# Joining the output weights in another order in a decoder layer's prologue, one core of a Trainium2 chip

## The chip, the cores and the metric

The kernel runs on one core of one Trainium2 chip. A core has TensorE (PE, matmul; its weight loads are listed apart as PEld), VectorE (DVE), ScalarE (ACT), GpSimd (POOL) and SyncE (SP), which here only issues DMAs. The metric is the device time of one execution in microseconds (us); less is better.

## What is computed

A decoder layer over 16 batches of 100 tokens of width 512, in float32: a sliding-window attention with a learned sink, a cross attention over a context, and a mixture of 32 experts (top 4) with a shared expert. The part that matters here is how the attention's output is projected, and what it normalises first:

```
h = layernorm(x)
q = h @ wq_comp @ wq_up                     # 16 heads of 128
k = rmsnorm(rope(h @ wk)) ; v = h @ wv
attn = softmax(mask(q k^T) with sink) @ v
x1 = einsum('btgi,gio->btgo', attn as 4 groups of 512, out_w1)   # 4 groups
x1 = x1.reshape(b, t, 2048) @ out_w2        # (2048, 512)
x  = x + x1
...
x = x + cross_attention(layernorm(x), ctx)
x = x + experts(layernorm(x))
```

## The kernel before

Since nothing stands between `out_w1` and `out_w2`, the kernel multiplies the two once, ahead of the batches. This is the prologue. For each of 16 heads n a "join" makes a 128 x 512 product of four matmuls of 512 columns in bank n % 4 of the PSUM tensor W; ScalarE copies it to `wch` (the high half, counted by the semaphore `high`), VectorE subtracts to get `wcl` (the low half, counted by `low`), and TensorE counts finished joins on `wc_ps`. Joins 4g to 4g+3 need weight group g (2 MB: `w1T[g]` and `out_w2`'s rows). Groups 0 and 2 are loaded into the tile `w_x`, groups 1 and 3 into the tile `work` (the list `half`, L228). Join n waits for `low` of n - 3, as its bank must be free.

`work` also holds the attention's working tiles: the transposed queries `T16`, the probabilities `Pm` and `PX`, the rotated queries `qr`, and the normalised rows `h1`, `h2`. `resid` holds x for all 16 batches.

After the prologue `pipeline` runs `step(b)` on every engine. Step b does stage A for batch b (attention scores, softmax, output projection), stage Q for batch b + 1 (layer norm 1, compressed queries, keys, values, rotation), stage X for batch b - 1 (cross attention) and stage C for batch b - 2 (router). Step 0 has A for batch 0 and Q for batch 1. Batch 0's own Q stage stands in the prologue: `ln1_columns(0)` (four transposes of h1 into PSUM), `compress(0)`, `queries(0)` on TensorE, with `rotate_keys`, `rotate`, `norms`, `scale_keys` on VectorE and `squares` on ScalarE.

Each engine takes its instructions in the written order and waits in place. So does SP: its DMAs are issued in the order of its program, and a wait ahead of one holds back all behind it. SP's order is: group 0, x of batch 0, 14 constants, group 1, three attention weights; wait for 4 joins; group 2, x of batches 1 to 15; wait for 8 joins; group 3; wait for 12 joins; the cross attention's weights and the router (semaphore `ld_wx`); then three fills of DRAM (`pad_st`): the table of expert lists (L293), and zeros behind the rows of `hx_rows` (L294) and `out_rows` (L295); then the context of each step.

Layer norm 1 of batch b + 1 goes over three engines in step b. VectorE makes mean and variance (`ln_stats`, L1003 to L1007), GpSimd raises to the power -1/2 (`ln1`, L1323), VectorE applies it (`ln1_apply`, L1012). GpSimd's program begins so:

```python
wait_alone(pool, s.wqk, 1)
ln1(0)
qk(0)
pool.wait_ge(s.pad_st, 48)
pipeline(pool, step)
```

The wait on `pad_st` stands ahead of step 0's `ln1(1)`, and is met when all three fills have landed.

Of the kernel before, what the change touches and what calls it, by code (L numbers as in the profile page):

```python
# [8 lines left out]
NH, D = 16, 128  # L9
# [8 lines left out]
QH = 4  # L18
# [73 lines left out]
def build(nc, a, out):  # L92

    with ExitStack() as ctx:
# [132 lines left out]

        half = [[w_x[:, 0:2048], w_x[:, 2048:4096]], [work[:, 0:2048], work[:, 2048:4096]]]  # L228
        block = ctx.enter_context(nc.Block())
# [32 lines left out]
        def _(sp):  # L262
# [5 lines left out]
            for g in range(G):  # L268

                if g >= 2:  # L270
                    sp.wait_ge(s.wc_ps, 4 * (g - 1))
                h, done = half[g % 2], (s.ld_half0, s.ld_half1)[g % 2]
                sp.dma_start(h[0].rearrange("p (k n) -> p k n", k=4),
                             a["w1T"][g].rearrange("(k p) n -> p k n", p=P)).then_inc(done, 16)
                sp.dma_start(h[1].rearrange("p (k n) -> p k n", k=4),
                             a["out_w2"][GI * g:GI * (g + 1), :].rearrange("(k p) n -> p k n", p=P)).then_inc(done, 16)
                if g == 0:
                    sp.dma_start(rv[:, 0:1, :], xv[:, 0:1, :]).then_inc(s.ld_x0, 16)
                    for t, n in consts:
                        sp.dma_start(t[:, :], a[n]).then_inc(s.ld_const, 16)  # L280
                if g == 1:
                    for t, n, k in ((w_comp, "wq_comp", KC), (w_up, "wq_up", 1), (w_kv, "wkv", KC)):
                        sp.dma_start(t[:, :].rearrange("p (k n) -> p k n", k=k),
                                     a[n].rearrange("(k p) n -> p k n", p=P)).then_inc(s.ld_w, 16)
                if g == 2:
                    sp.dma_start(rv[:, 1:NB, :], xv[:, 1:NB, :]).then_inc(s.ld_x, 16)
            sp.wait_ge(s.wc_ps, 4 * (G - 1))
            for t, n, k in ((w_q, "WqT", KC), (w_kx, "WkvT", 1), (w_out, "WoutT", KC), (w_r, "routerT", KC)):
                sp.dma_start(t.rearrange("p (k n) -> p k n", k=k) if n != "routerT" else
                             t[:, :].rearrange("p (k n) -> p k n", k=k),  # L290
                             a[n].rearrange("(k p) n -> p k n", p=P)).then_inc(s.ld_wx, 16)

            sp.dma_start(table, a["c_table"]).then_inc(s.pad_st, 16)  # L293
            sp.dma_start(hx[NTOK:ROWS, :], a["c_zero"]).then_inc(s.pad_st, 16)  # L294
# [76 lines left out]
        def _(pe):  # L371
# [7 lines left out]

            def join(g):  # L380
                pe.wait_ge((s.ld_half0, s.ld_half1)[g % 2], 32 * (g // 2 + 1))
                for i in range(4):
                    n = 4 * g + i
                    if n >= 4:
                        pe.wait_ge(s.low, n - 3)
                    if n == 14:
                        pe.wait_ge(s.kv, 1)
# [10 lines left out]

            def ln1_columns(c):

                pe.wait_ge(s.ln1_h, c + 1)
                to_columns(wb[0], h1).then_inc(s.h1T_ps, 1)

            def compress(c):

                pe.wait_ge(s.h1T, c + 1)
                for k in range(KC):
                    last = mm(wb[1][:, 0:T], w_comp[:, P * k:P * (k + 1)], h1T[:, T * k:T * (k + 1)],
                              start=k == 0, stop=k == KC - 1)
                last.then_inc(s.hq_ps, 1)  # L410
                for k in range(KC):
                    last = mm(wb[2][0:T, 0:2 * D], h1T[:, T * k:T * (k + 1)], w_kv[:, 256 * k:256 * (k + 1)],
                              start=k == 0, stop=k == KC - 1)
                last.then_inc(s.kv_ps, 1)
# [15 lines left out]
            def step(b):  # L430
# [50 lines left out]
                if do.Q:  # L481
                    ln1_columns(b + 1)
                if do.X:
# [15 lines left out]
                if do.Q:  # L499
                    compress(b + 1)  # L500
                    pe.wait_ge(s.s_scaled, 4 * b + 4)
# [81 lines left out]

            for g in range(G - 1):
                join(g)
            pe.wait_ge(s.ld_const, 16 * 14)
            pe.wait_ge(s.ld_w, 48)
            pe.wait_ge(s.low, 4 * (G - 1))
            ln1_columns(0)
            compress(0)  # L590
            queries(0)
            join(G - 1)
            pe.wait_ge(s.low, 4 * G)
            pe.wait_ge(s.ld_wx, 64)
            pe.wait_ge(s.h1T, 1)
            pipeline(pe, step)
# [133 lines left out]
        def _(act):  # L730
# [10 lines left out]

            def ln1_columns(c):
                act.wait_ge(s.h1T_ps, c + 1)
                act.wait_ge(s.kv_ps, c)
                copy(h1T[:, :], wb[0][:, 0:QW]).then_inc(s.h1T, 1)

            def compressed(c):
                act.wait_ge(s.hq_ps, c + 1)
                act.wait_ge(s.q_ps, 4 * c)
                copy(hqT[:, :], wb[1][:, 0:T]).then_inc(s.hqT, 1)  # L750
# [3 lines left out]
                copy(kvs[:, :], wb[2][0:T, 0:2 * D]).then_inc(s.kv, 1)  # L754

# [29 lines left out]
            def step(b):  # L785
# [13 lines left out]
                if do.X:  # L799
# [10 lines left out]
                    copy(qpT[:, :], wb[1][:, 0:QW]).then_inc(s.qp, 1)  # L810
                if do.Q:
                    ln1_columns(b + 1)
                if do.A:
# [3 lines left out]
                    act.wait_ge(s.p_den, 2 * b)  # L817
                    fn(esink[:, :], sdiff[:, :], ACT.Exp).then_inc(s.e_sink, 1)
                if do.X:
                    act.wait_ge(s.sx_ps, b)  # L820
# [4 lines left out]
                if do.Q:  # L825
                    compressed(b + 1)
                    key_square(b + 1)
# [36 lines left out]

            joined(range(0, 12))
            ln1_columns(0)
            compressed(0)
            key_square(0)
            squares_first(0)
            queries_out(0)  # L870
            squares(0)
            joined(range(12, 16))
            pipeline(act, step)
# [105 lines left out]
        def _(dve):  # L979
# [74 lines left out]
            def step(b):  # L1054
                do = stages(b)
                if do.Q:
                    if isinstance(b, int) and b == 0:
                        dve.wait_ge(s.ld_x, 16)
                    ln_stats(0, b + 1, s.ln1_stats, s.ln1_var)
# [17 lines left out]
                if do.A:  # L1077
                    dve.wait_ge(s.s_max, 2 * b + 2)
                    tt(P3, P3, per_head(mx[:, :], NH), ALU.subtract).then_inc(s.s_shift, 1)
                    tt(sdiff[:, :], sink[:, :], mx[:, :], ALU.subtract).then_inc(s.s_sink, 1)  # L1080
                if do.C:

# [119 lines left out]
            ln1_apply(0)  # L1202
            joined(range(0, 12))
            rotate_keys(0)
            rotate(0)
            norms(0)
            scale_keys(0)
            joined(range(12, 16))
            pipeline(dve, step)
# [271 lines left out]
```

## Time and profile before

| | us |
|---|---|
| median of 3 runs | 1243.26 (1242.33 to 1248.41) |
| the profiled execution's own time | 1251.86 |
| its span (first to last instruction) | 1250.0 |
| TensorE busy | 1156.1 (92% of the span) |
| VectorE busy | 812.8 (65%) |
| ScalarE busy | 593.8 (48%) |
| GpSimd busy | 370.6 (30%) |

Times in the rows are counted from the span's start. The profiled execution is 8.6 us longer than the median of the runs, so differences are worked out on the profile and laid on either time.

### The profile page before, as it was taken

Reading aid. Unit: us, or ns where it says so; the run is one execution under the profiler, and the core shown is the slowest. Engines: PE = TensorE matmul, PEld = TensorE weight load, DVE = VectorE, ACT = ScalarE, POOL = GpSimd, SP = SyncE. Lnnn points to the kernel's source line nnn. Section 1 sums busy time; section 2 is a strip of 40 time slices with the busy share of each in tenths; the row PEclk is TensorE's granted clock in tenths of the full one; section 3 lists DMA queues with packets and bytes.
Section 4 is the critical chain, followed back from the end, with each engine's and each line's share of the span. In section 5 each row is a group of like instructions: output and inputs, shape, how many; then the busy total and the mean of one; then the engine's idle time right before and its main releaser. Section 6 shows DMA issues by size and latency. Waiting matters only on the chain. (4 is left out here: it accounts for less than half of the span.)

```text
span 1250.0 us, 20961 instructions
## 1 busy us (share of the span) xinstructions
PE 1156.1 (92%) x7761; PEld 911.6 (73%) x7762; DVE 812.8 (65%) x1392; ACT 593.8 (48%) x1402; POOL 370.6 (30%) x279
## 2 busy tenths in 40 slices
PE   7989999999999999999999874899989999999992
PEld 3456677767776777677767653888779988889992
DVE  1155698789878988898889754532266666655660
ACT  1234554465445554555456422411156666656661
POOL 0011102212221222121212111401226566665662
PEclk9989999999999999999999895899989999989997
DMA  7910000000000000000000008202569999999964
GB/s 267 244 72 2 1 9 9 15 14 8 9 15 14 8 9 15 14 8 9 15 14 8 10 14 219 67 27 63 181 210 274 267 271 268 272 264 246 267 116 59
DMA packets 70459, 121.10 MB, mean 97 GB/s; under 512 B 18502, under 2 KB 22134, under 8 KB 70250
## 3 DMA queue, kind: packets, MB, share of 16 engines
q1 hardware_dynamic: 52682, 82.46, 20.4%
q0 software_dynamic: 17728, 37.97, 14.6%
q8 instruction: 33, 0.54, 0.2%
q14 instruction: 16, 0.13, 0.0%
HBM read 93.55 MB, written 28.13 MB: 97 GB/s over the span
## 5 line engine op out<-in xcount | busy, mean ns | idle before, releaser
L1323 POOL TENSOR_TENSOR rall<-qkv_var,phalf 100x17 f32<-100x17 f32 x16 | 49.2, 3074 | 415.4 <-DVE qkv_var L1046 415.4
L1389 POOL DMA_INDIRECT out_rows<-work,idx x64 | 127.9, 1998 | 113.4 <-issue 87.2
L375 PE MATMUL QS<-xh,wh 128*128 128x256 f32 x512 | 148.6, 290 | 0.0
L376 PE MATMUL QS<-xl,wh 128*128 128x256 f32 x512 | 146.0, 285 | 0.0
L377 PE MATMUL QS<-xh,wl 128*128 128x256 f32 x512 | 145.9, 285 | 0.0
L375 PE MATMUL W<-wch,oth 128*100 128x512 f32 x256 | 104.9, 410 | 0.0
L376 PE MATMUL W<-wcl,oth 128*100 128x512 f32 x256 | 100.7, 393 | 0.0
L377 PE MATMUL W<-wch,otl 128*100 128x512 f32 x256 | 100.4, 392 | 0.0
L376 PEld LDWEIGHTS QS<-xl,wh 128*128 128x128 f32 x512 | 99.4, 194 | 1.2
L375 PEld LDWEIGHTS QS<-xh,wh 128*128 128x128 f32 x512 | 99.4, 194 | 1.2
L377 PEld LDWEIGHTS QS<-xh,wl 128*128 128x128 f32 x512 | 99.2, 194 | 0.0
L1271 DVE TENSOR_TENSOR wl<-raw,wh 128x2048 fp32r<-128x2048 f32 (+1 forms) x48 | 84.5, 1760 | 12.6 <-ACT wh L734 12.2
L1323 POOL TENSOR_TENSOR rstd<-var,phalf 100x1 f32<-100x1 f32 (+1 forms) x48 | 30.4, 632 | 201.9 <-DVE var L1007 127.1
L1353 POOL DMA_INDIRECT expert_lists<-tok,slot x64 | 74.3, 1161 | 24.2 <-issue 18.4
L1292 DVE TENSOR_TENSOR work<-work,QS 128x256 f32<-128x256 f32 x64 | 26.8, 418 | 76.2 <-ACT work L946 74.2
L734 ACT ACTIVATE wh<-raw 128x2048 fp32r<-128x2048 f32 (+1 forms) x48 | 70.8, 1475 | 0.0
L734 ACT ACTIVATE work<-W 128x400 f32<-128x400 f32 (+1 forms) x128 | 54.2, 509 | 31.7 <-PE W L515 31.6
L478 PEld LDWEIGHTS W<-h2T,w_x 128*128 128x128 f32 x512 | 59.7, 192 | 8.0 <-issue 7.5
L926 ACT ACTIVATE work<-W,wcol 128x512 f32<-128x512 f32 x64 | 40.6, 686 | 46.7 <-PE W L377 43.0
L580 PE MATMUL W<-w_x,oxT 128*100 128x512 f32 x128 | 60.8, 619 | 0.0
L734 ACT ACTIVATE work<-QS 100x400 f32<-100x400 f32 (+1 forms) x80 | 43.8, 611 | 34.1 <-DVE work L1038 23.3
L478 PE MATMUL W<-h2T,w_x 128*128 128x100 f32 x512 | 59.4, 274 | 0.0
(206 smaller groups left out, 2874.8 us busy)
## 6 DMA issues: line engine op xcount, KB each, us to landing
raw<-in_w SPq DMA_DIRECT2D x24, 1024.0 KB
raw<-in_w SPq DMA_DIRECT2D x24, 512.0 KB
work<-in_w SPq DMA_DIRECT2D x8, 1024.0 KB
work<-in_w SPq DMA_DIRECT2D x8, 512.0 KB
hx_rows<-h3x SPq DMA_DIRECT2D x16, 212.5 KB
h_columns<-h3s SPq DMA_DIRECT2D x16, 200.0 KB, 1.9
h3T<-h_columns SPq DMA_DIRECT2D x16, 200.0 KB, 4.7
out_rows<-ytiles POOLq DMA_DIRECT2D x16, 200.0 KB, 2.5
```

What stands on the lines that cost most here:

```text
L375: mm(dst, ah, bh, start=start, stop=False)
L376: mm(dst, ah, bl, start=False, stop=False)
L377: return mm(dst, al, bh, start=False, stop=stop)
L478: last = mm(wb[1][:, T * i:T * (i + 1)], w_q[:, 512 * k + P * i:512 * k + P * (i + 1)], h2T[:, T * k:T * (k + 1)], start=k == 0, stop=k == ...
L580: last = mm(wb[3][0:T, :], oxT[:, T * k:T * (k + 1)], w_out[:, 512 * k:512 * (k + 1)], start=k == 0, stop=k == KC - 1)
L734: return fn(dst, src, ACT.Copy)
L926: last = fn(Y[e % 2][:, 512 * j:512 * (j + 1)], wb[j][:, :], ACT.Copy, scale=wcol[e % RING][:, j:j + 1])
L1271: tt(wl[e % 2][:, c], slots_w[e % RING][:, c], wh[e % 2][:, c].bitcast(fp32), ALU.subtract).then_inc(m.wl, 1)
L1292: tt(ea[:, 256 * v:256 * (v + 1)], et[:, 256 * v:256 * (v + 1)], QS[:, 1280 + 512 * v:1536 + 512 * v], ALU.mult).then_inc(m.act, 1)
L1323: return nc.gpsimd.tensor_tensor(out=dst, in0=src, in1=phalf[:, 0:src.shape[1]], op=ALU.pow)
L1353: nc.gpsimd.indirect_dma_start(table, on_rows(slot[:, k:k + 1]), tok[:, :], None)\
L1389: nc.gpsimd.indirect_dma_start(out, on_rows(idx[:, NE * j + e:NE * j + e + 1]), Y[e % 2][:, 512 * j:512 * (j + 1)], None, compute_op=ALU.a ...
```

## The change

Four things are done together.

1. Weight groups 1 and 3 no longer land in `work`, but in the places of x's rows 8 to 15 in `resid` (columns 4096 to 8191). So `work` is free for batch 0 while joins run.
2. x is loaded in two parts. Batches 1 to 7 are issued right after group 1 and the attention weights, with no wait. Batches 8 to 15 are issued when all 16 joins are done (`wc_ps` at NH = 16, since the last group lies in their place), after the cross attention's weights.
3. Batch 0's Q stage goes among the joins, in the banks of QS in place of W: its transposes after join 7, `compress(0)` after join 8, `queries(0)` after join 9. VectorE's and ScalarE's parts are put between their halves of the joins.
4. Joins 14 and 15 go from the prologue into step 0, after its scores on TensorE. Their evictions stand on ScalarE on both sides of the softmax's exponentials, and on VectorE behind the softmax's subtraction.

The diff, without the passing of banks as arguments:

```diff
-        half = [[w_x[:, 0:2048], w_x[:, 2048:4096]], [work[:, 0:2048], work[:, 2048:4096]]]
+        half = [[t[:, 0:2048], t[:, 2048:4096]] for t in (w_x, resid[:, HID * NB // 2:HID * NB])]
@@ SP
-                if g == 2:
-                    sp.dma_start(rv[:, 1:NB, :], xv[:, 1:NB, :]).then_inc(s.ld_x, 16)
+                if g == 1:
+                    sp.dma_start(rv[:, 1:NB // 2, :], xv[:, 1:NB // 2, :]).then_inc(s.ld_x, 16)
             sp.wait_ge(s.wc_ps, 4 * (G - 1))
...
+            sp.wait_ge(s.ld_x, 16)
+            sp.wait_ge(s.wc_ps, NH)
+            sp.dma_start(rv[:, NB // 2:NB, :], xv[:, NB // 2:NB, :]).then_inc(s.ld_x, 16)
             sp.dma_start(table, a["c_table"]).then_inc(s.pad_st, 16)
             sp.dma_start(hx[NTOK:ROWS, :], a["c_zero"]).then_inc(s.pad_st, 16)
             sp.dma_start(out[NTOK:ROWS, :], a["c_zero"][:, 0:HID]).then_inc(s.pad_st, 16)
@@ PE, step
                 if do.Q:
-                    ln1_columns(b + 1)
+                    if isinstance(b, int) and b == 0:
+                        pe.wait_ge(s.qT, QH)
+                        join(range(14, 16))
+                    ln1_columns(b + 1, wb[0])
...
                 if do.Q:
-                    compress(b + 1)
+                    if isinstance(b, int) and b == 0:
+                        pe.wait_ge(s.low, NH)
+                    compress(b + 1, wb)
@@ PE, prologue
-            for g in range(G - 1):
-                join(g)
+            join(range(0, 8))
             pe.wait_ge(s.ld_const, 16 * 14)
+            ln1_columns(0, qb[0])
+            join(range(8, 9))
             pe.wait_ge(s.ld_w, 48)
-            pe.wait_ge(s.low, 4 * (G - 1))
-            ln1_columns(0)
-            compress(0)
+            compress(0, qb)
+            join(range(9, 10))
+            pe.wait_ge(s.kv, 1)
             queries(0)
-            join(G - 1)
-            pe.wait_ge(s.low, 4 * G)
+            join(range(10, 14))
+            pe.wait_ge(s.low, 14)
             pe.wait_ge(s.ld_wx, 64)
-            pe.wait_ge(s.h1T, 1)
             pipeline(pe, step)
@@ ACT, step
-                if do.Q:
-                    ln1_columns(b + 1)
+                first = isinstance(b, int) and b == 0
+                if first:
+                    joined(range(14, 15))
+                if do.Q and not first:
+                    ln1_columns(b + 1, wb[0])
                 if do.A:
                     act.wait_ge(s.s_shift, b + 1)
                     fn(Pm[0:T, :], Pm[0:T, :], ACT.Exp).then_inc(s.p_exp, 1)
                     act.wait_ge(s.s_sink, b + 1)
                     act.wait_ge(s.p_den, 2 * b)
                     fn(esink[:, :], sdiff[:, :], ACT.Exp).then_inc(s.e_sink, 1)
+                if first:
+                    joined(range(15, 16))
+                    ln1_columns(b + 1, wb[0])
@@ DVE, step
-                    if isinstance(b, int) and b == 0:
-                        dve.wait_ge(s.ld_x, 16)
+                    if isinstance(b, int) and b < 2:
+                        dve.wait_ge(s.ld_x, 16 * (b + 1))
...
                     tt(sdiff[:, :], sink[:, :], mx[:, :], ALU.subtract).then_inc(s.s_sink, 1)
+                    if isinstance(b, int) and b == 0:
+                        joined(range(14, 16))
```

What SP issues from group 2 on, before the change (the brackets are the semaphores that a row waits for):

```order
L273 DMA w_x<-in_w1T 128x4x512 [waits wc_ps]
L275 DMA w_x<-in_out_w 128x4x512
L286 DMA resid<-in_x 100x15x512
L273 DMA work<-in_w1T 128x4x512 [waits wc_ps]
L275 DMA work<-in_out_w 128x4x512
L289 DMA w_x<-in_WqT 128x4x512 [waits wc_ps]
L289 DMA w_x<-in_WkvT 128x1024
L289 DMA w_x<-in_WoutT 128x4x512
L289 DMA w_r<-in_routerT 128x4x32
L293 DMA expert_lists<-in_c_table 16x3328
L294 DMA hx_rows<-in_c_zero 16x8704
L295 DMA out_rows<-in_c_zero 256x512
```

And after it, from the same place:

```order
L286 DMA resid<-in_x 100x7x512
L273 DMA w_x<-in_w1T 128x4x512 [waits wc_ps]
L275 DMA w_x<-in_out_w 128x4x512
L273 DMA resid<-in_w1T 128x4x512 [waits wc_ps]
L275 DMA resid<-in_out_w 128x4x512
L289 DMA w_x<-in_WqT 128x4x512 [waits wc_ps]
L289 DMA w_x<-in_WkvT 128x1024
L289 DMA w_x<-in_WoutT 128x4x512
L289 DMA w_r<-in_routerT 128x4x32
L295 DMA resid<-in_x 100x8x512 [waits wc_ps,ld_x]
L296 DMA expert_lists<-in_c_table 16x3328
L297 DMA hx_rows<-in_c_zero 16x8704
```

The zeros of `out_rows` come next (L298). The three fills now stand behind x of batches 8 to 15 and its wait for the sixteenth join.

TensorE from the end of the prologue, through the scores of step 0, before the change:

```order
L390 MATMUL W<-work 128x512 [waits low]
L390 MATMUL W<-work 128x512 x3
L438 MATMUL QS<-ident,kr 128x100 [waits k_scaled,h1T,q_rot,ld_wx,low]
L449 MATMUL W<-ident,work 128x100 x16
L455 MATMUL QS<-mask_115,identb 100x400 [waits qT,kT]
```

Behind those scores, before the change:

```order
L458 MATMUL QS<-kT,work 100x100 x4
L396 MATMUL W<-ident,work 128x100 [waits ln1_h]
L396 MATMUL W<-ident,work 128x100 x3
L408 MATMUL W<-h1T,w_comp 128x100 [waits h1T]
L408 MATMUL W<-h1T,w_comp 128x100 x3
L412 MATMUL W<-w_kv,h1T 100x256 x4
```

And after the change, in the same place:

```order
L460 MATMUL QS<-kT,work 100x100 x4
L392 MATMUL W<-resid 128x512 [waits low,ld_half1,qT]
L392 MATMUL W<-resid 128x512 x3
L392 MATMUL W<-resid 128x512 [waits low,ld_half1]
L392 MATMUL W<-resid 128x512 x3
L398 MATMUL W<-ident,work 128x100 [waits ln1_h]
L398 MATMUL W<-ident,work 128x100 x3
L410 MATMUL W<-h1T,w_comp 128x100 [waits h1T,low]
L410 MATMUL W<-h1T,w_comp 128x100 x3
L414 MATMUL W<-w_kv,h1T 100x256 x4
```

The two last joins now stand between batch 0's scores and batch 1's transposes, and the compression waits for `low` too.

GpSimd's first rows after the change, which are those of before with other line numbers:

```order
L1344 TENSOR_TENSOR rstd_88<-var_85,phalf 100x1 [waits ln1_var]
L1344 TENSOR_TENSOR rall<-qkv_var,phalf 100x17 [waits s_scaled,qk_var]
L1344 TENSOR_TENSOR rstd_88<-var_85,phalf 100x1 [waits ln1_var,pad_st]
L1344 TENSOR_TENSOR rall<-qkv_var,phalf 100x17 [waits s_scaled,qk_var]
L1344 TENSOR_TENSOR rstd_89<-var_86,phalf 100x1 [waits ln2_var]
```

The third row is batch 1's layer norm. Nothing moved here; its wait for the fills is unchanged.

## Rows read from the trace of the kernel before

**Rows 1.** Busy time by stretch: start:end, length, engines (instructions), PE clock, DMA share, GB/s.

```profile
140.00:600.00 460.00, 458.30 (x3369) 336.57 (x3369) 385.06 (x715) 246.02 (x771) 94.79 (x84) 1.00 0.04 11
```

**Rows 2.** Timeline of TensorE: start, length, line, tiles, records [idle before <-releaser].

```profile
39.28 13.90 PE L390 MATMUL W<-w_x 128*128 128x512 f32 x32
...
54.79 0.53 PE L396 MATMUL W<-ident,work 100*128 100x100 f32 x4 [1.62 <-DVE wcl L997]
...
63.59 13.90 PE L390 MATMUL W<-work 128*128 128x512 f32 x32
78.90 0.30 PE L438 MATMUL QS<-ident,kr 100*128 100x100 f32 x1 [1.41 <-DVE wcl L997]
...
83.21 0.87 PE L458 MATMUL QS<-kT,work 128*100 128x100 f32 x8
87.27 0.93 PE L396 MATMUL W<-ident,work 100*128 100x100 f32 x4 [3.19 <-DVE work L1012]
88.80 2.03 PE L408 MATMUL W<-h1T,w_comp 128*128 128x100 f32 x8 [0.59 <-ACT h1T L734]
...
93.65 3.60 PE L419 MATMUL QS<-w_up,hqT 128*100 128x512 f32 x8
97.08 1.54 PE L515 MATMUL W<-ident,work 100*100 100x100 f32 x16
...
127.52 1.14 PE L408 MATMUL W<-h1T,w_comp 128*128 128x100 f32 x8
...
130.22 3.60 PE L419 MATMUL QS<-w_up,hqT 128*100 128x512 f32 x8
```

**Rows 3.** Timeline of SP: start and length of the issue of a DMA.

```profile
39.47 0.37 SPq L273 DMA_DIRECT2D work<-in_w1T  x1
...
53.20 0.37 SPq L289 DMA_DIRECT2D w_x<-in_WqT  x1
...
63.02 0.59 SPq L295 DMA_DIRECT2D out_rows<-in_c_zero  x1
```

**Rows 4.** DMA issues, 0 to 90 us: count, KB each, median us to landing.

```profile
resid<-in_x SPq DMA_DIRECT2D x1, 3000.0 KB
...
w_x<-in_out_w SPq DMA_DIRECT2D x2, 1024.0 KB, 7.6
...
hx_rows<-in_c_zero SPq DMA_DIRECT2D x1, 544.0 KB, 5.6
...
out_rows<-in_c_zero SPq DMA_DIRECT2D x1, 512.0 KB, 8.6
```

**Rows 5.** Busy time by stretch in the prologue and step 0, columns as in the first group.

```profile
23.00:24.00 1.00, 1.00 (x4) 0.52 (x3) 0.64 (x1) 0.00 (x0) 0.00 (x0) 1.00 0.00 0
34.00:41.00 7.00, 7.00 (x18) 3.04 (x17) 1.38 (x2) 1.20 (x2) 0.00 (x0) 1.00 0.66 136
51.00:54.00 3.00, 2.17 (x6) 0.63 (x4) 0.26 (x2) 0.60 (x1) 0.00 (x0) 1.00 0.67 214
56.00:62.00 6.00, 6.00 (x21) 4.30 (x22) 0.69 (x5) 1.83 (x11) 0.00 (x0) 0.74 1.04 392
88.00:93.00 5.00, 4.41 (x16) 3.52 (x15) 3.38 (x6) 2.40 (x4) 0.00 (x0) 0.50 0.02 5
```

**Rows 6.** Timeline of GpSimd around batch 1's layer norm.

```profile
80.10 0.56 POOL L1323 TENSOR_TENSOR rstd<-var,phalf 100x1 f32<-100x1 f32 x1 [5.97 <-DVE var L1007]
```

**Rows 7.** Timeline of VectorE there.

```profile
86.67 0.54 DVE L1012 TENSOR_SCALAR work<-resid,mv,rstd 100x512 f32<-100x512 f32 x1
```

**Rows 8.** Timeline of ScalarE there.

```profile
77.52 0.60 ACT L734 ACTIVATE wch<-W 128x512 fp32r<-128x512 f32 x1 [2.83 <-PE W L390]
...
88.24 0.50 ACT L734 ACTIVATE h1T<-W 128x400 f32<-128x400 f32 x1 [6.97 <-PE W L396]
88.98 1.54 ACT L815 ACTIVATE work<-work 100x1600 f32<-100x1600 f32 x1 [0.24 <-DVE work L1079]
90.42 0.20 ACT L818 ACTIVATE esink<-sdiff 100x16 f32<-100x16 f32 x1
```

More of the change, by code:

```diff
@@ L377, in split_product, with join @@
                 return mm(dst, al, bh, start=False, stop=stop)
[L380 to L383, printed above, removed]
+            def join(heads):
+                for n in heads:
+                    g, i = n // 4, n % 4
+                    pe.wait_ge((s.ld_half0, s.ld_half1)[g % 2], 32 * (g // 2 + 1))
                     if n >= 4:
                         pe.wait_ge(s.low, n - 3)
-                    if n == 14:
-                        pe.wait_ge(s.kv, 1)
                     for k in range(4):
@@ L397, in to_columns, with ln1_columns, compress @@
                 return last
-            def ln1_columns(c):
+            def ln1_columns(c, bank):
                 pe.wait_ge(s.ln1_h, c + 1)
-                to_columns(wb[0], h1).then_inc(s.h1T_ps, 1)
-            def compress(c):
+                to_columns(bank, h1).then_inc(s.h1T_ps, 1)
+            def compress(c, banks):
                 pe.wait_ge(s.h1T, c + 1)
                 for k in range(KC):
-                    last = mm(wb[1][:, 0:T], w_comp[:, P * k:P * (k + 1)], h1T[:, T * k:T * (k + 1)],
+                    last = mm(banks[1][:, 0:T], w_comp[:, P * k:P * (k + 1)], h1T[:, T * k:T * (k + 1)],
                               start=k == 0, stop=k == KC - 1)
@@ L411, in compress @@
                 for k in range(KC):
-                    last = mm(wb[2][0:T, 0:2 * D], h1T[:, T * k:T * (k + 1)], w_kv[:, 256 * k:256 * (k + 1)],
+                    last = mm(banks[2][0:T, 0:2 * D], h1T[:, T * k:T * (k + 1)], w_kv[:, 256 * k:256 * (k + 1)],
                               start=k == 0, stop=k == KC - 1)
@@ L740, in joined, with ln1_columns, compressed @@
                     copy(wch[:, 512 * n:512 * (n + 1)], wb[n % 4]).then_inc(s.high, 1)
-            def ln1_columns(c):
+            def ln1_columns(c, bank):
                 act.wait_ge(s.h1T_ps, c + 1)
                 act.wait_ge(s.kv_ps, c)
-                copy(h1T[:, :], wb[0][:, 0:QW]).then_inc(s.h1T, 1)
-            def compressed(c):
+                copy(h1T[:, :], bank[:, 0:QW]).then_inc(s.h1T, 1)
+            def compressed(c, banks):
                 act.wait_ge(s.hq_ps, c + 1)
                 act.wait_ge(s.q_ps, 4 * c)
-                copy(hqT[:, :], wb[1][:, 0:T]).then_inc(s.hqT, 1)
+                copy(hqT[:, :], banks[1][:, 0:T]).then_inc(s.hqT, 1)
                 act.wait_ge(s.kv_ps, c + 1)
@@ L753, in compressed @@
                 act.wait_ge(s.k_rot, c)
[L754 removed]
+                copy(kvs[:, :], banks[2][0:T, 0:2 * D]).then_inc(s.kv, 1)
             def queries_out(c):
@@ L825, in step @@
                 if do.Q:
-                    compressed(b + 1)
+                    compressed(b + 1, wb)
                     key_square(b + 1)
@@ L863, in step @@
                     copy(oxT[:, :], wb[1][:, 0:QW]).then_inc(s.oxT, 1)
-            joined(range(0, 12))
-            ln1_columns(0)
-            compressed(0)
+            joined(range(0, 8))
+            ln1_columns(0, qb[0])
+            joined(range(8, 9))
+            compressed(0, qb)
             key_square(0)
+            joined(range(9, 10))
             squares_first(0)
             queries_out(0)
+            joined(range(10, 11))
             squares(0)
-            joined(range(12, 16))
+            joined(range(11, 14))
             pipeline(act, step)
@@ L1202, in _ @@
             ln1_apply(0)
-            joined(range(0, 12))
+            joined(range(0, 9))
             rotate_keys(0)
+            joined(range(9, 10))
             rotate(0)
+            joined(range(10, 12))
             norms(0)
+            joined(range(12, 13))
             scale_keys(0)
-            joined(range(12, 16))
+            joined(range(13, 14))
             pipeline(dve, step)
```

## The prediction

> **What bounds the kernel now.** I read the busy time by stretch first, then TensorE's timeline over the prologue and step 0, then what SP issues and when it lands, and last the three engines that make batch 1's layer norm. In the loop over the batches TensorE is busy 458.3 of 460 us [rows 1]: each step is paced by TensorE, the steps follow each other without slack, and so what moves the start of the steady run moves the end by as much. The change touches only what lies ahead of it. Nothing behind step 1 is altered, so I follow one milestone: the start of step 0's probability transposes, 97.08 us before [rows 2]. From there on the work is the same.
>
> How that milestone comes about now: joins 8 to 11 run back to back from 39.28, 3.43 us each (each group of four is 13.90 long with its tail, and starts of one kind repeat that spacing) [rows 2]. Then batch 0's Q stage stands alone, with joins held back until 63.59, so it costs about 10.4 us of TensorE's time; joins 12 to 15 follow, and step 0 starts at 78.90. Its scores end at 84.08. TensorE then idles until VectorE has applied batch 1's layer norm (86.67) and starts its transposes at 87.27, compression at 88.80, queries at 93.65 [rows 2, 7]. In 88 to 93 us it had the clock at 0.50, the 1.2 GHz level [rows 5].
>
> **What the change takes away.** With Q among the joins no join waits for it. TensorE's work up to the end of join 11 is then 39.28 + four joins (13.73) + columns (0.5) + compression at the full clock (127.52 to 130.22: 2.70) + queries (93.65 to 97.08: 3.43) = 59.6 us [rows 2]. Joins 12 and 13 take it to 66.5. Step 0 started 1.4 us behind its last join before [rows 2], which gives 67.9. VectorE and ScalarE keep up: a join's eviction is 0.60 us [rows 8] against 3.43 of a join, and what they do for Q takes about as long as before and lies under three to four joins.
>
> Step 0 also waits for the cross attention's weights. They were issued at 53.20, behind the twelfth join [rows 3], and will be at 59.6. A pair of 1 MB loads with nothing in front needs 8.0 us from the first issue (0.4 to the second, 7.6 to landing) [rows 4]; the four loads hold 0.6 MB more, 1.5 us at 392 GB/s [rows 5]. They land at about 69.1, so step 0 starts at 69.2, 9.7 us earlier than now. TensorE has idled 2.7 us by then, near the 3.19 us behind which the half clock stood before [rows 2, 5]; I take it that the clock falls and costs 2 us over the next four (at either level known: 0 or 2). Scores end at 69.2 + 5.2 + 2 = 76.4, joins 14 and 15 at 83.3.
>
> The early load of x and the new places of groups 1 and 3 I cost at nothing. x of batches 1 to 7 (7/15 of 3000 KB, 1.43 MB [rows 4]) is now in front of group 2, and even at 136 GB/s [rows 5] takes 10.5 us. The loads up to the attention weights are through before 23 us, where the DMA share is 0.00 [rows 5]; x starts there, group 2 gets the engines that x uses at 33 and needs 5.4 us at 392 GB/s more: about 38.5, and join 8 wants it at 39.8. If this cover of 1.3 us is missing, the excess is paid once. Group 3 no longer stands behind x and has 12 us to spare.
>
> **What the change adds.** The step that I follow closely is SP's. The three fills were issued just behind the cross weights, the last at 63.02, landed 8.6 us later at 71.6 [rows 3, 4], and GpSimd, which waits for them ahead of batch 1's power, ran it at 80.10 as soon as VectorE's variance was there [rows 6]: the wait cost nothing. Now the fills stand behind x of batches 8 to 15, and that waits for the sixteenth join, which is inside step 0. So at 83.3 us SP issues x, then the fills. From issue to full landing there are: 2.7 us of start and completion (the pair above, 8.0 us less 2.1 MB at 392 GB/s); x, 1.64 MB; the fills, 544 and 512 KB and a table of 16 x 3328 words, 1.29 MB, 3.3 us at 392 GB/s [rows 4, 5]. x loads go slower than others: alone from 34 to 41 us the core moved 136 GB/s with a DMA share of 0.66, that is 10.6 of 16 engines, and 214 with 0.67 from 51 to 54 [rows 5]. I weigh the two by their length, 159 GB/s, so x takes 10.3 us (7.7 to 12.0). The fills must be whole on all engines, those that x holds too. They have landed at 83.3 + 2.7 + 10.3 + 3.3 = 99.6.
>
> The Trainium skill (DMA: Bandwidth & Descriptors, Specifications) gives about 27 GiB/s for one DMA engine. Ten engines would carry x at some 290 GB/s, an estimate from that page, and x would take 5.7 us in place of 10.3; the sum below would be 12.2 in place of 16.8. The rows of x, 13.6 to 21.4 GB/s on an engine, do not reach that.
>
> Queued behind it: GpSimd cannot make batch 1's power (0.56 us), VectorE waits in place for it with the softmax's subtraction of batch 0 behind, ScalarE with the exponentials behind that, TensorE with the transposes. Batch 1's layer norm is applied at 99.6 + 0.56 + 0.15 = 100.3 in place of 86.67: +13.6 [rows 6, 7].
>
> From there the way is longer too. Before, compression began 2.1 us behind the layer norm (86.67 to 88.80) [rows 2, 7], with h1T copied ahead of the exponentials (88.24, then 88.98) [rows 8]. Now ScalarE copies h1T behind them: subtraction as before, so exponentials 2.3 us behind the layer norm, 1.64 us for both, join 15's eviction 0.60, h1T 0.50 [rows 8], 0.2 of handing over: 5.2 us. That adds 3.1. TensorE is cold, as before (0.50 from 88 to 93 [rows 5]), so compression and queries cost the same 8.3 us. Join 15's low half on VectorE ends just with h1T and delays nothing more; the softmax's last multiplication ends some 4 us ahead of the transposes.
>
> **The sum.** 13.6 + 3.1 = +16.7, with rounding +16.8: the milestone goes from 97.1 to 113.9. On the profiled execution, span 1250.0 and own time 1251.86, that is 1268.7; on the median, 1243.26, it is 1260.1. The 8.6 us between the two are the profiled execution's own and are not in my forecast, which is 1260 us.
>
> **Rivals.**
> *Faster, the reordering pays.* If GpSimd's wait did not come last, TensorE would go on at 83.3 with the transposes; join 15's eviction, h1T and its low half let the compression start at 84.6, warm, 2.70 and 3.43 later the milestone stands at 90.7: -6.4, 1236.9 us. What speaks for it is that TensorE's stand-alone Q stage does vanish. It needs the fills landed by about 82.8, where +0 lies at 83.5 for the layer norm's start plus 13.6; they are issued at 83.3 at the earliest. It decides only if the fills are not behind the join. The order rows say that they are. Within 0.5% needs the fills by 89.
> *x runs fast.* If the ten engines carry x at the rate of one in the full stream, 392/16 = 24.5 GB/s each [rows 5], x takes 6.7 us and the sum is 13.2, 1256.5. Of x's own rows none shows it. This is also where the page's figure would lead. If in addition the clock does not fall in front of step 0, it is 11.2, 1254.5.
> *The transfers collide.* If group 2 is late for join 8 by 2 us, and the fills need the 8.6 us of their landing before in place of 6.0, the sum is 16.8 + 2 + 2.6 = 21.4, 1264.7.
> *All near the best.* x and the fills at 392 GB/s with the clock kept: 7.5 + 2.7 us from 81.3, the sum is 8.7, 1252.0.
>
> **How the numbers follow.** Forecast 0.62; x fast 0.16; collision 0.11; all near the best 0.04; faster 0.03; less than 0.5% either way, by a landing that I cannot derive, 0.04. The range is 1252 to 1266: it takes in the bounds of x's rate, both levels of the clock and the collision. What a measurement can tell here is about 0.5%, 6.2 us, so faster 0.03, within it 0.04, slower 0.93.
>
> **What would show it.** In the changed kernel's profile: joins without a pause from 8.7 to about 66 us; step 0's first matmul near 69; x and the fills issued at about 83; GpSimd's second small power idle until about 100, with VectorE's layer norm right behind it; TensorE idle from 83 to 101 and cold after; the transposes near 114. I am wrong if that power runs before 90, or if the span behind it is longer or shorter than before.

## The result, and the profile after

The changed kernel is slower: 1264.46 us (median of 4 runs, 1261.77 to 1267.32) against 1242.8 us (4 runs, 1235.7 to 1248.41); the ratio is 1.0178, 95% interval 1.0119 to 1.0237. The ratios here and below leave out every execution more than 1.5% above the fastest of its kernel, so they need not be the quotient of the medians. By this ratio the change costs 22 us (15 to 29). Its profiled execution took 1266.37 us, with a span of 1264.5, 14.5 more than the profiled one of before. The forecast was 1260, in a range of 1252 to 1266.

First TensorE's timeline, the same stretch as [rows 2]:

```profile
38.72 0.51 PE L398 MATMUL QS<-ident,work 100*128 100x100 f32 x4
...
42.52 1.03 PE L410 MATMUL QS<-h1T,w_comp 128*128 128x100 f32 x8
...
48.55 3.60 PE L421 MATMUL QS<-w_up,hqT 128*100 128x512 f32 x8
...
58.85 7.03 PE L392 MATMUL W<-resid 128*128 128x512 f32 x16
68.76 0.40 PE L440 MATMUL QS<-ident,kr 100*128 100x100 f32 x1 [2.88 <-issue]
68.95 2.87 PE L451 MATMUL W<-ident,work 100*128 100x100 f32 x16
...
76.61 7.05 PE L392 MATMUL W<-resid 128*128 128x512 f32 x16
100.64 0.93 PE L398 MATMUL W<-ident,work 100*128 100x100 f32 x4 [16.98 <-DVE work L1028]
105.26 2.03 PE L410 MATMUL W<-h1T,w_comp 128*128 128x100 f32 x8 [3.69 <-DVE wcl L1013]
...
109.69 3.60 PE L421 MATMUL QS<-w_up,hqT 128*100 128x512 f32 x8
113.13 1.54 PE L522 MATMUL W<-ident,work 100*100 100x100 f32 x16
```

Read it in two halves. Up to 83.7 the change does what it says: batch 0's queries lie among the joins, no join waits, and step 0 starts at 68.76 where it started at 78.90 [rows 2]. Then TensorE stands still for 17 us, until VectorE has applied the layer norm. The milestone of the prediction, the start of step 0's probability transposes, is at 113.13 in place of 97.08.

Why VectorE is late stands one engine further, in the queues of SP and GpSimd and in VectorE's own timeline:

```profile
83.75 0.32 SPq L295 DMA_DIRECT2D resid<-in_x  x1
84.11 0.68 SPq L296 DMA_DIRECT2D expert_lists<-in_c_table  x1
84.83 0.57 SPq L297 DMA_DIRECT2D hx_rows<-in_c_zero  x1
85.45 0.59 SPq L298 DMA_DIRECT2D out_rows<-in_c_zero  x1
```

```profile
99.45 0.56 POOL L1344 TENSOR_TENSOR rstd<-var,phalf 100x1 f32<-100x1 f32 x1 [35.41 <-DMA out_rows<-in_c_zero]
```

```profile
68.20 0.15 DVE L1023 TENSOR_SCALAR var<-mv 100x1 f32<-100x1 f32 x1
...
100.04 0.55 DVE L1028 TENSOR_SCALAR work<-resid,mv,rstd 100x512 f32<-100x512 f32 x1 [20.60 <-POOL rstd L1344]
100.50 1.82 DVE L1095 TENSOR_TENSOR work<-work,mx 100x1600 f32<-100x1600 f32 x1
...
104.51 0.69 DVE L1013 TENSOR_TENSOR wcl<-W,wch 128x512 fp32r<-128x512 f32 x1 [1.51 <-ACT wch L741]
```

The variance was ready at 68.35. GpSimd's power of 0.56 us could have run then; it ran at 99.45, and its releaser is the last of the three fills, `out_rows<-in_c_zero`. In [rows 6] the same instruction was released by VectorE's variance at 80.10. From the issue of x at 83.75 to the power are 15.7 us. What the engines and the DMA did in them, and ScalarE behind them:

```profile
84.00:99.00 15.00, 0.00 (x0) 0.00 (x0) 0.00 (x0) 0.00 (x0) 0.00 (x0) 0.65 0.67 199
```

```profile
102.36 1.54 ACT L825 ACTIVATE work<-work 100x1600 f32<-100x1600 f32 x1 [21.49 <-DVE work L1095]
103.80 0.20 ACT L828 ACTIVATE esink<-sdiff 100x16 f32<-100x16 f32 x1
103.90 0.58 ACT L741 ACTIVATE wch<-W 128x512 fp32r<-128x512 f32 x1
104.38 0.50 ACT L741 ACTIVATE h1T<-W 128x400 f32<-128x400 f32 x1
```

No engine computes anything for 15 us while 3 MB are moved. Behind it ScalarE makes h1T only after the exponentials and join 15's eviction, and VectorE's half of join 15 stands behind that eviction too. Compression starts 5.2 us behind the layer norm (100.04 to 105.26), where it was 2.1. What ends its wait is join 15's low half (104.51 and 0.69 long, up to 105.20); h1T was ready 0.3 us earlier.

### The profile page after: what moved, and what is told of

It reads as the page before. It is cut to its first block and busy times, and to the rows that moved or that the text cites. A ratio compares the mean times of both kernels' runs of the same rounds, so it can differ in the third digit from the quotient of the medians.

```text
span 1264.5 us, 20973 instructions
## 1 busy us (share of the span) xinstructions
PE 1158.4 (92%) x7761; PEld 915.0 (72%) x7762; DVE 812.1 (64%) x1392; ACT 594.3 (47%) x1402; POOL 360.5 (29%) x279
## 3 DMA queue, kind: packets, MB, share of 16 engines
q1 hardware_dynamic: 52692, 82.46, 20.2%
## 5 line engine op out<-in xcount | busy, mean ns | idle before, releaser
L1410 POOL DMA_INDIRECT out_rows<-work,idx x64 | 121.8, 1904 | 123.4 <-issue 81.8
```

What stands on the lines that cost most here:

```text
L1410: nc.gpsimd.indirect_dma_start(out, on_rows(idx[:, NE * j + e:NE * j + e + 1]), Y[e % 2][:, 512 * j:512 * (j + 1)], None, compute_op=ALU.a ...
```

## The experiments

The theory (A): all of the loss comes from the fills' new place in SP's queue, behind the sixteenth join and x, since GpSimd waits for them ahead of batch 1's layer norm. Against it: the joins inside step 0 and their evictions are what costs (B); something behind the milestone costs too (C); the transfers disturb, not the wait (E). Three smaller questions go with them: do the fills delay the cross weights (D), do the fills alone take the time from issue to power (F), and does the milestone of before vary by chance (G).

The table has each kernel's milestone, the same instruction's start in the last full step (15), and the total. The profile of before had 97.08 and 710.32, that of the changed kernel 113.13 and 726.38. The kernels were timed in three groups, each beside the kernel before, and the ratio is to before in the same group. Before had a median of 1244.19 us (29 runs) in the first group (changed again, fills first, GpSimd waits later, before with the second half of x and the fills late), 1243.44 (29) in the second (before again, fills between, weights' wait later, joins in prologue) and 1247.64 (7) in the third (evictions ahead). So medians of different groups are not to be compared with each other.

| kernel | milestone | step 15 | median us (runs) | ratio to before, 95% |
|---|---|---|---|---|
| before, again | 95.49 | 708.72 | 1244.31 (10) | 1.0003 (0.9969 to 1.0036) |
| changed, again | 114.08 | 728.90 | 1262.75 (6) | 1.0189 (1.0135 to 1.0244) |
| changed, fills first | 88.41 | 701.59 | 1241.02 (12) | 0.9992 (0.9944 to 1.0041) |
| changed, GpSimd waits later | 90.81 | 703.99 | 1238.23 (12) | 0.9998 (0.9959 to 1.0037) |
| before, second half of x and fills late | 101.80 | 715.00 | 1250.73 (12) | 1.0069 (1.0035 to 1.0102) |
| changed, fills between | 106.57 | 719.77 | 1257.01 (4) | 1.0119 (1.0058 to 1.0180) |
| fills first, weights' wait later | 87.18 | 703.52 | 1239.73 (12) | 0.9949 (0.9915 to 0.9983) |
| fills first, joins in prologue | 93.94 | 707.18 | 1240.87 (12) | 0.9995 (0.9956 to 1.0033) |
| changed, evictions ahead | 112.22 | 728.68 | 1266.97 (4) | 1.0130 (1.0086 to 1.0173) |

**The changed kernel again.**

> The changed kernel once more, beside the others of this group. The milestone (start of step 0's probability transposes) was 97.08 us before and 113.13 in the changed kernel's profile, +16.05, while the medians of four runs each lie 21.7 us apart. Theory A (the fills stand behind the sixteenth join, GpSimd waits for them, and nothing behind the milestone differs) expects +16 us, 1259 where the kernel before has 1243. Theory C (something behind the milestone costs too) expects +20 or more and a milestone that again moves by only 16.

The power ran at 100.53, again released by the last fill, and the milestone was 114.08. Between the milestones of step 0 and step 1 lie 38.2 us here and 36.6 in the first profile; the 1.6 are in step 1's scores, where some matmuls ran slow. The milestone moved by 17.0 us against the first profile of before and the medians by 18.6, between what A and C expect, so this run alone decides nothing between them.

```profile
133.53 1.50 PE L460 MATMUL QS<-kT,work 128*100 128x100 f32 x8
134.82 0.54 PE L457 MATMUL QS<-mask,identb 100*100 100x400 bf16 x1
135.15 1.54 PE L460 MATMUL QS<-kT,work 128*100 128x100 f32 x8
136.48 0.54 PE L457 MATMUL QS<-mask,identb 100*100 100x400 bf16 x1
136.82 0.95 PE L460 MATMUL QS<-kT,work 128*100 128x100 f32 x8
137.61 0.34 PE L457 MATMUL QS<-mask,identb 100*100 100x400 bf16 x1
137.78 0.87 PE L460 MATMUL QS<-kT,work 128*100 128x100 f32 x8
```

One group of eight takes 0.87 us at the full clock and 1.54 at half.

**The fills issued first.**

```diff
-            sp.wait_ge(s.ld_x, 16)
-            sp.wait_ge(s.wc_ps, NH)
-            sp.dma_start(rv[:, NB // 2:NB, :], xv[:, NB // 2:NB, :]).then_inc(s.ld_x, 16)
             sp.dma_start(table, a["c_table"]).then_inc(s.pad_st, 16)
             sp.dma_start(hx[NTOK:ROWS, :], a["c_zero"]).then_inc(s.pad_st, 16)
             sp.dma_start(out[NTOK:ROWS, :], a["c_zero"][:, 0:HID]).then_inc(s.pad_st, 16)
+            sp.wait_ge(s.ld_x, 16)
+            sp.wait_ge(s.wc_ps, NH)
+            sp.dma_start(rv[:, NB // 2:NB, :], xv[:, NB // 2:NB, :]).then_inc(s.ld_x, 16)
```

> The changed kernel with the three fills issued ahead of x of batches 8 to 15 and its wait for the sixteenth join, nothing else. Theory A: the fills land near 71 us, GpSimd's second small power runs at about 68.5 to 72, joins 14 and 15 still end at 83.5, compression starts warm at about 84.7 and the milestone is at 90.5 to 91, so -6 us against before and -22 against the changed kernel. Theory B (the cost is the two joins in step 0 and their evictions around the exponentials, which hold h1T): most of the +16 stays. Theory D (the fills delay the cross weights when they are issued near them): step 0 starts at 71 or later in place of 68.8.

```profile
68.81 0.28 PE L440 MATMUL QS<-ident,kr 100*128 100x100 f32 x1 [2.98 <-issue]
68.93 1.54 PE L451 MATMUL W<-ident,work 100*128 100x100 f32 x16
...
73.81 7.05 PE L392 MATMUL W<-resid 128*128 128x512 f32 x16
80.70 0.51 PE L398 MATMUL W<-ident,work 100*128 100x100 f32 x4
82.28 1.14 PE L410 MATMUL W<-h1T,w_comp 128*128 128x100 f32 x8 [1.07 <-DVE wcl L1013]
83.25 1.89 PE L414 MATMUL W<-w_kv,h1T 128*100 128x256 f32 x8
84.98 3.60 PE L421 MATMUL QS<-w_up,hqT 128*100 128x512 f32 x8
88.41 1.54 PE L522 MATMUL W<-ident,work 100*100 100x100 f32 x16
```

GpSimd's power ran at 72.00, still released by the fills but hidden under the joins, and the milestone is 24.7 us earlier than the changed kernel's. That settles A against B: both joins and their evictions are where the change put them. Step 0 started at 68.81, so the fills do not delay the cross weights. Against before the milestone is 7.1 to 8.7 us earlier, more than the 6 expected, because this execution kept the full clock across a pause of 2.98 us (16 transposes in 1.54 us) where the changed kernel's lost it across one of 2.88 (2.87 us). The total gives the loss back: the ratio is 0.9992 where the changed kernel had 1.0189 in the same group. The gain over before it does not show: the medians lie 3.2 us apart, the interval reaches from -0.56% to +0.41%, and the 7.1 to 8.7 us would be 0.57 to 0.70%, just outside it.

**GpSimd's wait moved, the transfers left alone.**

```diff
             qk(0)
-            pool.wait_ge(s.pad_st, 48)
...
                     power(rstd[2][:, :], var[2][:, :]).then_inc(s.ln3_rstd, 1)
+                if isinstance(b, int) and b == 1:
+                    pool.wait_ge(s.pad_st, 48)
```

> The changed kernel with SP's order kept, but GpSimd's wait for the fills moved from ahead of step 0 to the end of its step 1, ahead of its first use of the table. The fills still land near 99 us behind x. Theory A: the same -6 us against before as with the fills first, milestone 90.5 to 91. Theory E (it is the transfers themselves between 84 and 99 us that slow the engines or the batch's start, not the wait): the loss stays or shrinks only in part, since these transfers run exactly as in the changed kernel.

The power ran at 69.34 and the milestone is at 90.81, as expected. x and the fills were issued at 83.36 and moved 201 GB/s under a working TensorE:

```profile
84.00:99.00 15.00, 14.32 (x66) 9.47 (x67) 10.25 (x18) 6.60 (x22) 0.00 (x0) 1.00 0.66 201
```

Set it beside the line of the changed kernel above: the same DMA share and rate, TensorE busy 14.32 us in place of none. From the compression to the milestone it took 6.13 us (84.68 to 90.81) with the transfers running, and 6.13 with the fills issued first (82.28 to 88.41). The transfers disturb nothing there; E falls.

**Before, with the second half of x and the fills issued late.** x of batches 1 to 7 stays behind group 2, where all of x was.

```diff
-                    sp.dma_start(rv[:, 1:NB, :], xv[:, 1:NB, :]).then_inc(s.ld_x, 16)
+                    sp.dma_start(rv[:, 1:NB // 2, :], xv[:, 1:NB // 2, :]).then_inc(s.ld_x, 16)
...
+            sp.wait_ge(s.ld_x, 16)
+            sp.wait_ge(s.wc_ps, NH)
+            sp.dma_start(rv[:, NB // 2:NB, :], xv[:, NB // 2:NB, :]).then_inc(s.ld_x, 16)
             sp.dma_start(table, a["c_table"]).then_inc(s.pad_st, 16)
...
-                    if isinstance(b, int) and b == 0:
-                        dve.wait_ge(s.ld_x, 16)
+                    if isinstance(b, int) and b < 2:
+                        dve.wait_ge(s.ld_x, 16 * (b + 1))
```

> The kernel before with only SP's new order: x of batches 8 to 15 in a load of its own behind the wait for the sixteenth join, the fills behind it; joins, queries and places as before. The sixteenth join ends at about 77.5, and from issue to GpSimd's power the changed kernel took 15.7 us (83.75 to 99.45). Theory A: the power runs at 93.3 in place of 80.1, the layer norm at 93.9 in place of 86.7, and the milestone and the whole move by +7.2 us. Theory B: no more than +1, since no join and no eviction has moved.

```profile
91.06 0.56 POOL L1326 TENSOR_TENSOR rstd<-var,phalf 100x1 f32<-100x1 f32 x1 [19.57 <-DMA out_rows<-in_c_zero]
```

Without one join moved, the kernel is slower by 0.69% (0.35 to 1.02), 8.6 us. From issue (74.93) to power are 16.1 us. The milestone is +4.7 to +6.3 against the two profiles of before, less than the +7.2 expected, and B's +1 falls. The power was earlier than the expected 93.3 because here step 0 started 2.7 us ahead of the first profile of before, with the same work in front of it: 1.1 us it was ahead at batch 0's transposes already (53.68 and 54.79), and the rest came behind them, where its compression ran at the full clock.

**Before again.**

> The kernel before once more, for a second profile. Its one profile had TensorE at the half clock from 56 to 59 us, in batch 0's compression, which the profile of the kernel before with SP's new order had not, with the same work there and a step 0 that started 2.7 us earlier. Theory G (which of the two an execution gets is chance, and the milestone of before varies by some 2 us): this profile may show the milestone at 94 to 95 in place of 97.1. Then the changed kernel is up to 19 us behind before, and the medians' 18 to 21 need nothing behind the milestone. Theory C (something behind the milestone): the milestone is 97 again.

```profile
55.00:60.00 5.00, 4.45 (x21) 3.01 (x22) 0.69 (x5) 2.23 (x11) 0.00 (x0) 1.00 1.03 388
```

The same window of the first profile of before:

```profile
55.00:60.00 5.00, 4.41 (x20) 3.61 (x19) 0.00 (x0) 0.76 (x2) 0.00 (x0) 0.66 1.04 370
```

Clock 1.00 in the one, 0.66 on average in the other, and the milestone at 95.49 in place of 97.08. So one profile's milestone is known to some 2 us only. G stands. With both profiles of before and both of the changed kernel, the shift up to step 15 is 16.1 to 20.2 us, mean 18.1. That lies inside both intervals of the total (15 to 29 us in the result, 17 to 30 in the repetition), so C is not needed, but it is not excluded either: the ratios stand for 22.1 and 23.5 us. In five of the other seven altered kernels as well the total by the ratio is 1.7 to 6.9 us above the shift at step 15 (against the mean of the two profiles of before); in two it is 0.3 and 3.0 below. A cost of a few us behind step 15 is neither shown nor ruled out.

**The fills behind the join, but ahead of x.**

```diff
             sp.wait_ge(s.ld_x, 16)
             sp.wait_ge(s.wc_ps, NH)
-            sp.dma_start(rv[:, NB // 2:NB, :], xv[:, NB // 2:NB, :]).then_inc(s.ld_x, 16)
             sp.dma_start(table, a["c_table"]).then_inc(s.pad_st, 16)
             sp.dma_start(hx[NTOK:ROWS, :], a["c_zero"]).then_inc(s.pad_st, 16)
             sp.dma_start(out[NTOK:ROWS, :], a["c_zero"][:, 0:HID]).then_inc(s.pad_st, 16)
+            sp.dma_start(rv[:, NB // 2:NB, :], xv[:, NB // 2:NB, :]).then_inc(s.ld_x, 16)
```

> The changed kernel with the three fills behind the wait for the sixteenth join, as there, but ahead of x of batches 8 to 15 in place of behind it. This takes x's own transfer out of GpSimd's wait and leaves the join in it. Theory A, by the sum's terms (2.7 us of start and completion and 3.3 us of bytes from the issue at 83.7): the power runs at about 89.7 in place of 99.45, and the milestone is 9.7 us earlier than the changed kernel's 113.1, at 103.4, still some 6 us or more behind the kernel before. Theory F (nearly all of the 15.7 us is the completion of fills in DRAM, not x in front of them): the power stays at 95 or later.

```profile
92.03 0.56 POOL L1344 TENSOR_TENSOR rstd<-var,phalf 100x1 f32<-100x1 f32 x1 [27.55 <-DMA out_rows<-in_c_zero]
```

The landing of the last fill, first in the changed kernel, then here:

```profile
out_rows<-in_c_zero SPq DMA_DIRECT2D x1, 512.0 KB, 13.9
out_rows<-in_c_zero SPq DMA_DIRECT2D x1, 512.0 KB, 6.1
```

The first fill was issued at 84.55, 7.5 us before the power. So of the 15.7 us the place behind x is worth 8.2: F falls, and A's split holds in kind. The 8.2 are not x's own time. Where x ran without the fills, it was slower: in the kernel with the fills first it moved

```profile
83.00:92.00 9.00, 9.00 (x43) 5.60 (x43) 4.48 (x11) 4.87 (x18) 0.00 (x0) 1.00 0.68 171
```

and here, behind the fills, 182 GB/s from 93 to 99 us, which is 9.0 to 9.6 us for its 1.64 MB. In the changed kernel x and the fills overlapped in part: the table of expert lists, issued behind x at 84.11, had landed 7.3 us later, at 91.4, and the DMA share was 1.10 from 87 to 89, where x alone holds 0.68. The milestone is 6.6 us earlier than the changed kernel's, less than the 9.7 forecast: the fills took 1.5 us more, they were issued 0.8 later, and the way from the power to the milestone was 14.5 us in place of 13.7.

**The wait for the cross weights moved to their first use.**

```diff
             pe.wait_ge(s.low, 14)
-            pe.wait_ge(s.ld_wx, 64)
...
                     to_columns(wb[0], h2).then_inc(s.h2T_ps, 1)
+                    if isinstance(b, int) and b == 1:
+                        pe.wait_ge(s.ld_wx, 64)
```

> The changed kernel with the fills first (as in the run of that name), and TensorE's wait for the cross attention's weights moved from ahead of step 0 to step 1, ahead of their first use. TensorE no longer idles 2.9 us behind join 13 but 1.4, as before the change: step 0 starts 1.3 to 1.5 us earlier, and the clock does not fall there, which cost 2 to 3 us where it did. Milestone 86.5 to 88; total 1.5 to 4 us less than with the fills first. If the weights are late for something else, step 1 shows TensorE waiting for them and the gain is gone.

Step 0's transposes started at 67.69, the milestone is 87.18, and this is the one version whose interval lies below that of before: -0.51% (-0.85 to -0.17). It is faster than the changed kernel too, as are all versions with GpSimd's wait out of the way. In its profile 3.1 us went again in step 1, where the 16 transposes and the scores behind them ran at the half clock:

```profile
105.17 2.87 PE L451 MATMUL W<-ident,work 100*128 100x100 f32 x16
```

The weights are not what held step 1: TensorE waited 2.43 us ahead of it for VectorE's rotated keys, and 2.42 in the kernel with the fills first. This profiled execution was also the longest of its twelve (1246.96). Against the fills first, timed in another group, the intervals of the ratios overlap, so what this one edit is worth in the total stays unresolved.

**Joins 14 and 15 back in the prologue.** The diff undoes their calls in the three engines' step 0 and extends the prologue's ranges to 16.

> The changed kernel with the fills first, and joins 14 and 15 with their evictions back in the prologue, as before the change: only the queries among the joins and the new places of groups 1 and 3 are left. Step 0 starts at about 74.8 (joins end at 73.4, 1.4 to hand over), VectorE's layer norm stands some 7.8 us behind it, TensorE idles 3.2 us there again and goes on cold or not. Milestone 91 to 93, which is 2.5 to 4.5 us later than with the joins inside step 0, and 2 to 4 earlier than before. Theory B (the joins inside step 0 cost more than they hide): the milestone is no later than with them inside.

```profile
83.75 0.93 PE L398 MATMUL W<-ident,work 100*128 100x100 f32 x4 [3.19 <-DVE work L1017]
```

The pause of 3.19 us behind the scores is back, to the hundredth that of [rows 2]. The milestone is 93.94, 0.9 us later than the expected range, as step 0 started 0.6 later: 1.6 to 3.1 us ahead of before, and 3.1 to 5.5 behind the two versions with the joins inside. Of the 5.5 against the fills first, which differs in nothing else, some 2 to 3 would be gone if the clock had fallen there ahead of step 0, as in the other profiles with that pause. B falls here too, at the milestone: the joins inside step 0 hide what they were put over, once nobody else is late. The totals (0.9995 and 0.9992) do not tell the two apart.

**The evictions ahead of the softmax.** The changed kernel again, but with a new place for the evictions: ScalarE's `joined(range(14, 16))` and `ln1_columns` now stand ahead of the exponentials, VectorE's `joined(range(14, 16))` ahead of `ln1_apply`.

> The changed kernel, SP's order and GpSimd's wait as there, with both evictions of joins 14 and 15 and the copy of h1T ahead of the softmax: on ScalarE ahead of the exponentials, on VectorE ahead of the layer norm's application. It tests the sum's second term, the 3.1 us by which compression stands further behind the layer norm than before (5.2 us in place of 2.1), against the rival that this distance is set by something else, TensorE's clock for one. If the term is right, compression starts some 2.1 us behind the layer norm again and the milestone is at 110 in place of 113.1 to 114.1, the total 3 us less than the changed kernel's, near 1260. If not, the distance stays near 5 us.

```profile
101.36 0.93 PE L398 MATMUL W<-ident,work 100*128 100x100 f32 x4 [17.30 <-DVE work L1026]
102.98 2.00 PE L410 MATMUL W<-h1T,w_comp 128*128 128x100 f32 x8 [0.69 <-ACT h1T L741]
104.77 3.62 PE L414 MATMUL W<-w_kv,h1T 128*100 128x256 f32 x8
108.18 4.21 PE L421 MATMUL QS<-w_up,hqT 128*100 128x512 f32 x8
112.22 1.54 PE L522 MATMUL W<-ident,work 100*100 100x100 f32 x16
```

```profile
100.76 0.55 DVE L1026 TENSOR_SCALAR work<-resid,mv,rstd 100x512 f32<-100x512 f32 x1 [15.34 <-POOL rstd L1342]
```

Compression starts 2.2 us behind the layer norm (100.76), so the term's mechanism is as stated. But only 1.6 of the 3.0 us reach the milestone: compression and queries took 9.2 us, where the changed kernel's took 7.9, as the clock came back later in the work. So the milestone is at 112.2 and not at 110. Step 1 then lost 3.2 us at the half clock in this execution. The total decides nothing: the median of 1266.97 is above the changed kernel's, but it stands beside a before of 1247.64, and the ratio, 1.0130 (1.0086 to 1.0173), is below the changed kernel's 1.0178 and 1.0189 with overlapping intervals. The expected 3 us less is neither shown nor refuted.

## Why the prediction was right

The path was right: the fills behind the sixteenth join, GpSimd's wait for them, VectorE, ScalarE and TensorE queued behind it. Some of the closeness of its numbers is luck, as the terms show.

- **Joins and queries.** Join 11 ended at 58.9 (forecast 59.6), step 0 started at 68.8 (69.2), the clock fell across that pause and joins 14 and 15 ended at 83.7 (83.3). Group 2 landed 12.2 us behind its issue at 25.6, at 37.8 (38.5), and join 8 did not wait. The fall of the clock was taken from a single row. It came out in five of the six profiles that had this pause (2.8 to 3.1 us), this one among them; with the fills first the clock did not fall. It cost 1.7 to 3.2 us against the 5.0 that step 0 takes up to its joins at the full clock, where the forecast had 2.
- **The wait for the fills.** Forecast 99.6, measured 99.45 at the power. That it is so close is luck: the sum laid start, x and fills end to end, 2.7 + 10.3 + 3.3 us. Having x in front made the wait 8.2 us longer, where the sum had 10.3, and the fills with start and completion cost 7.5 in place of 6.0. The rate of x was not the error, or a small one: forecast at 159 GB/s, it moved 171 and 182 where it ran without the fills. The term was too long because x and the fills overlap in part, and the term of the fills too short. The Trainium skill (DMA: Bandwidth & Descriptors, Specifications) gives about 27 GiB/s for one engine; by the estimate from it, x would take 5.7 us. Measured are 17 to 18 GB/s on each of ten engines, and the measurement decides.
- **The longer way behind the layer norm.** Forecast 5.2 us to the compression, measured 5.2. The prediction had join 15's low half end just with h1T; it ended 0.3 us behind it and was what the compression waited for. With both evictions ahead of the softmax the distance is 2.2 us again, so the distance is explained. That all of its 3.1 us reaches the end is not shown: of 3.0 us, 1.6 were left at the milestone.
- **The sum.** Milestone forecast +16.8, measured +16.05 on the first pair of profiles and 18.6 on the second. The medians of the result are 21.7 us apart and those of the repetition 18.6; the forecast of 1260 was 4.5 below the median. Up to 1.6 of it can be the first profile of before, which had the slower prologue of two, and up to 1.6 more step 1, which lost the clock in one of the two profiles of the changed kernel and which the sum left out. The rest is within what the runs can tell, and its cause is open. The span behind the milestone, which was to stay the same, went from 1152.9 to 1151.4 us on the first pair of profiles and from 1146.5 to 1151.0 on the second.
- **The rivals.** "Faster, the reordering pays" is what the fills first and the later wait on GpSimd make of the milestone. Its price was given as -6.4, and GpSimd's later wait, where the clock fell too, has a milestone 6.3 earlier than the first profile of before and 4.7 earlier than the second. Its first condition holds, that GpSimd's wait does not come last. The second, that the fills are not behind the join, is only one way to that: with GpSimd's later wait they are still behind it. The median is nearest to the price of the collision (1264.7), but group 2 was not late, and the fills took 1.5 us more than forecast in place of 2.6. Of the fast x, the term (6.7) was 1.5 below the measured 8.2, though x did not run at its rate.

The totals of the two versions with GpSimd's wait out of the way and nothing else moved do not show their gain of 5 to 9 us at the milestone. The profiles agree from the milestone to step 15 (613.2 us in eight of eleven, 614.8 to 616.5 in three whose step 1 ran in part at the half clock), but from there to the end they spread from 519.9 to 541.2 us, with no order by kernel. A part of that spread lies in the experts: in the last 320 to 341 us TensorE waited for gathers of rows out of `hx_rows`, 7.0 to 12.3 us in all in ten of the profiles, and not at all in the shortest, that of GpSimd's later wait. Why the gathers were late in one execution and not in another stays open.

## What to carry to other kernels

A wait that costs nothing is held at nothing by the place of what it waits for in another engine's queue. When a step is moved behind a new wait in a queue, list everything that stands behind it there, and for each the first instruction in program order that waits for it, also where that wait looks unrelated: here fills of which the first is needed in step 2 held a layer norm in step 0, one instruction of 0.56 us, and no engine computed for 15 us. And before an early milestone is taken from one profile, a second profile of the same kernel tells how far chance alone moves it: here by 1.6 us, most of it the clock.

## What the runs showed of the hardware that was not expected

With near the same pause, 2.88 and 2.98 us, behind the same dense matmuls, TensorE's clock fell in one execution and stayed up in the other. Over all six profiles with this pause (2.77 to 3.06 us) it fell in five. The same holds for the kernel before, with pauses of 1.62 and 0.59 us around four transposes, where it fell in one profile of two, and for step 1, where it fell in three of the eleven profiles behind a pause of 2.43 us. Each such fall cost 1.5 to 3.2 us. Starting the same work earlier behind a long pause did not bring it back to the full clock as much earlier: of 3.0 us gained at the compression's start 1.6 were left three groups of matmuls later.

The second load of x (100 partitions, 2 KB of each of eight batches) moved 171 and 182 GB/s when it ran without the fills, at a DMA share of 0.68 and 0.67. Fills issued behind it on the same queue did not wait for its end: the table had landed at 91.4, when the core had moved 1.6 MB since 84 us, less than x and the table together (1.85 MB).
